# A convolution with dynamic per-channel weights on one core: the opening reordered, and the moments moved from GpSimd to TensorE and ScalarE

## The chip, the cores and the metric

The kernel runs on one core of a Trainium2 chip. The metric is the device time in microseconds of one execution, as the median of several. TensorE is written PE, VectorE DVE, ScalarE ACT, GpSimd POOL and SyncE SP, as in the profile. Each engine works through its own list of instructions in order and waits on semaphores; DMAs are all issued by SP.

## The reference

The input `x` has 16 images of 32 channels of 128x128, in float32. Each channel of each image is normalised over its pixels, then convolved 3x3 with a kernel of its own that is computed from the image's channel means, gated and added to the input:

```
v   = (x - mean(x)) / sqrt(var(x) + 1e-5)          # per image and channel
avg = v.mean(axis=(2, 3))
wk  = sigmoid(avg @ w1.T + b1)                      # 9 numbers per image and channel
y   = depthwise_conv3x3(v, wk, pad=1) + conv_bias
out = x + (v - y) * fscale * v + y
```

The mean of `v` is zero but for rounding; the kernel computes it nevertheless (`dev_mean`), since the reference's weights come from it.

## The kernel before, in words

**Layout.** A partition holds one row of 16-row blocks (stepped by 14 rows, so that neighbours overlap), a parity of columns and one of 4 slots of channels; the 32 channels are 8 groups of 4 slots. One image is 8 groups of 128x576 numbers (128x594 with margins). Everything below runs per image `i` and group `g`; a tile is one (i, g), and there are 128.

**The steady work of a tile.** ACT subtracts the mean in place (`centre`, L686) and later writes the linear part (`linear_part`, L722). PE does the convolution: 12 matmuls on 64x64 quarters of the array, 6 of 448 columns (`paired`, L435) and 6 of 128 (`halved`, L441), each run in two passes because the numbers are float32, into one of three PSUM tiles. DVE multiplies and adds out of PSUM (`product`, L582), which frees that PSUM tile: tile n starts on PE only when product n-3 is done. POOL adds the linear part for two groups at a time (`add_pair`, L852), and SP stores.

**The chain of an image.** Before tile (j, 0) can run, image j needs its statistics and its weights. DVE takes `bn` (L531) over each group and folds the pieces in `rows` (L538), for which ACT first scales the counts (`count`, L728). PE averages the row means (`mean_even`/`mean_odd`, L358/L364; `mean_whole`, L383, for images 0 and 1) and ACT negates them (`negative_mean`, L669). POOL then computes deviation, its square and the second moment (`second_moments`, L814, L817, L819). PE averages those (`spread_*`, L370, L377, L388), ACT copies them out (`copy_stats`, L690, L692), POOL takes the power -1/2 (`deviation`, L809) and lays out the averages (`average_columns`, L823, L825). PE spreads them (`averages`, L396, L411), ACT copies (`copy_averages`, L698), PE multiplies with the weights (`dynamics_*`, L404, L419, L427), ACT applies the sigmoid (L705), POOL scales (`scaled_taps`, L843), and DVE builds the 24 banded matrices for PE (`matrices`, L549, L556; for image 0 in four steps, `first_matrices`). PE's part of the chain for images i+1 and i+2 is put between the matmuls of image i by `chain(i, at)`: `at` is 2g before tile g, and 2g+1 in its middle.

**Order.** Nothing is planned at run time; the order on each engine is written out. For the steady images DVE alternates `bn(i+2 or i+3, .)` with `product(i, .)`, has `rows(i+2)` before product 2 and `matrices(i+1)` after product 4. In the opening DVE takes all of bn(0), rows(0), all of bn(1), rows(1), `first_matrices`, four of bn(2). PE waits for the constants before it does anything, and fills some gaps with idle matmuls (`keep_warm`, L497, 240 columns on 64 rows of the array). SP loads image 0 in four pieces, then the gates, the constants, the weights, images 1 to 4.

Of the kernel before, what the change touches and what calls it, by code (L numbers as in the profile page):

```python
# [13 lines left out]
TAPS = 3  # L14
# [20 lines left out]
WARM = 240  # L35

START_AHEAD, AHEAD = 4, 6
# [10 lines left out]
FIRST_LOADS = 4  # L48
# [6 lines left out]
for _name, _width in (("average", PARTS), ("band", TAPS * HALF), ("turn", TAPS),  # L55
                      ("spread", INPUTS), ("phase", PARTS), ("counts", 1)):
    _AT[_name] = (_N, _N + _width)
    _N += _width
# [13 lines left out]
def constants():  # L72
# [12 lines left out]
    put("average", same * new[:, None])  # L85
    put("counts", (row >= ROWS - STEP).astype(np.float32))
# [71 lines left out]
def build(nc, x, w1r, gate, const, out):  # L158
    with ExitStack() as ctx:
# [34 lines left out]
        row_stats = sb("row_stats", [PARTS, 2, GROUPS, 2])  # L194
        shift = sb("shift", [PARTS, 2, 2, GROUPS])
        moments = sb("moments", [PARTS, 2, GROUPS])
        square = sb("square", [PARTS, GROUPS])
# [26 lines left out]
        zstats_ps = stat_ps[:, GROUPS:3 * GROUPS]  # L224
        avg_ps = stat_ps[0:INPUTS, 128:128 + PARTS]
# [22 lines left out]
        dev_ready = sem("dev_ready")  # L248
        square_ready = sem("square_ready")
# [95 lines left out]
        def _(pe):  # L345
            pe.wait_ge(consts_loaded, 16)

# [4 lines left out]

            def mean_even(j):
                pe.wait_ge(rows_done, j + 1)
                for cols in (TOP, BOTTOM):
                    nc.tensor.matmul(stat_ps[cols, 0:GROUPS], average(TOP, cols), row_stats[TOP, j % 2, :, 0],  # L358
                                     start=True, stop=False).then_inc(mean_half, 1)

            def mean_odd(j):
                pe.wait_ge(mean_half, 2 * (j - 1))
                for cols in (TOP, BOTTOM):
                    nc.tensor.matmul(stat_ps[cols, 0:GROUPS], average(BOTTOM, cols), row_stats[BOTTOM, j % 2, :, 0],  # L364
                                     start=False, stop=True).then_inc(mean_done, 1)

            def spread_even(j):
                pe.wait_ge(moments_ready, j + 1)
                for cols in (TOP, BOTTOM):
                    nc.tensor.matmul(stat_ps[cols, GROUPS:3 * GROUPS], average(TOP, cols),  # L370
                                     moments[TOP].rearrange("p a g -> p (a g)"),
                                     start=True, stop=False).then_inc(zstats_half, 1)

            def spread_odd(j):
                pe.wait_ge(zstats_half, 2 * j)
                for cols in (TOP, BOTTOM):
                    nc.tensor.matmul(stat_ps[cols, GROUPS:3 * GROUPS], average(BOTTOM, cols),  # L377
                                     moments[BOTTOM].rearrange("p a g -> p (a g)"),
                                     start=False, stop=True).then_inc(zstats_done, 1)

            def mean_whole(j):
                pe.wait_ge(rows_done, j + 1)
                nc.tensor.matmul(mean_ps, const_of("average"), row_stats[:, j % 2, :, 0],  # L383
                                 start=True, stop=True).then_inc(mean_done, 1)

            def spread_whole(j):
                pe.wait_ge(moments_ready, j + 1)
                nc.tensor.matmul(zstats_ps, const_of("average"), moments[:].rearrange("p a g -> p (a g)"),  # L388
                                 start=True, stop=True).then_inc(zstats_done, 1)
# [4 lines left out]
            def averages_whole(j):  # L394
                pe.wait_ge(avg_cols_ready, j + 1)
# [71 lines left out]

            def chain(i, at):
                j = i + 1
                if j < B:  # L470
                    late = 3 if j <= 2 else 0
                    if at == 3 + late:
                        averages(j)
                    if at == 5 + late:
                        dynamics_first(j)
                    if at == 6 + late:
                        dynamics_second(j)
                if i == 0 and at == 1:
                    spread_even(1)
                if i == 0 and at == 2:  # L480
                    spread_odd(1)
                if i == 1 and at == 0:
                    spread_odd(2)
                j = i + 2
                if j < B:
                    if at == (11 if j == 2 else 9):
                        mean_even(j)
                    if at == (12 if j == 2 else 10):
                        mean_odd(j)
                    if at == (15 if j == 2 else 13):  # L490
                        spread_even(j)
                    if at == 14 and j > 2:
                        spread_odd(j)

            def keep_warm(count):
                for _ in range(count):
                    nc.tensor.matmul(conv_ps[:, CONV_TILES - 1, BANK:BANK + WARM], const_of("average")[0:HALF],  # L497
                                     cst[0:HALF, 0:WARM], start=True, stop=True)
# [28 lines left out]
        def _(dve):  # L527
# [6 lines left out]
            def rows(j):  # L534
                dve.wait_ge(pieces_done, GROUPS * (j + 1))
                dve.wait_ge(counted_ready, j + 1)
                for g in range(GROUPS):
                    ins = nc.vector.bn_aggr(row_stats[:, j % 2, g, :], pieces[:, j % 2, g].rearrange("p h s -> p (h s)"))  # L538
# [30 lines left out]
            def first_matrices():  # L569
                dve.wait_ge(tap_ready, 1)  # L570
                last_column(0)
                for k in range(PAIRS):
                    whole_triples(0, PAIR * k, PAIR * (k + 1))

# [39 lines left out]
            for i in range(B):  # L614
                nxt, stats = i + 1 < B, i + 2 < B
                if i == 0:
                    for g in range(START_AHEAD - 1):
                        bn(2, START_AHEAD + g)
                        product(0, g)
                    bn(2, GROUPS - 1)  # L620
                    product(0, 3)
                    rows(2)
                    bn(3, 0)
                    product(0, 4)
                    bn(3, 1)
                    product(0, 5)
                    bn(3, 2)
                    matrices(1)
                    product(0, 6)
                    bn(3, 3)  # L630
                    product(0, 7)
                    for g in range(4, AHEAD):
                        bn(3, g)
                else:
# [12 lines left out]
                    if nxt and i > 1:  # L647
# [4 lines left out]
                    if i == 1:  # L652
                        matrices(2)
# [8 lines left out]
        def _(act):  # L662
            act.wait_ge(ones_set, 1)
# [68 lines left out]
            count(0)  # L732
# [4 lines left out]
            centre(0, 1)  # L737
            centre(0, 2)
            copy_averages(0)
            centre(0, 3)  # L740
            centre(0, 4)
            sigmoid(0)
            count(1)
            for g in range(5, GROUPS):
                centre(0, g)
            negative_mean(1)
            fill_margins(1)
            for i in range(B):
                nxt, stats = i + 1 < B, i + 2 < B
                for g in range(GROUPS):  # L750
                    if nxt and g == (4 if i < 2 else 3):
                        copy_averages(i + 1)
                    if stats and g == (5 if i == 0 else 4):
                        count(i + 2)
                    if nxt and i > 1 and g == 5:
                        sigmoid(i + 1)
                    if stats and i > 0 and g == 6:
                        negative_mean(i + 2)
                        fill_margins(i + 2)
                    if i < 2 and g == 6:  # L760
                        sigmoid(i + 1)
                    if i == 0 and g == 7:
                        negative_mean(2)
                        fill_margins(2)
# [3 lines left out]
                    if i == 0 and g == 1:  # L768
                        copy_stats(1)
                    if i == 1 and g == 0:  # L770
                        copy_stats(2)
                    if stats and i > 0 and g == 7:
                        copy_stats(i + 2)

        @block.gpsimd
        def _(pool):
# [20 lines left out]
            pool.wait_ge(inv_ready, 1)  # L797
# [12 lines left out]

            def second_moments(j):
                pool.wait_ge(rows_done, j + 1)
                pool.wait_ge(neg_mean_ready, j + 1)
                nc.gpsimd.tensor_tensor(moments[:, 0], row_stats[:, j % 2, :, 0], neg_mean_of(j),  # L814
                                        ALU.add).then_inc(dev_ready, 1)
                pool.wait_ge(dev_ready, j + 1)
# [84 lines left out]
```

## Time and profile before

| what | value |
|---|---|
| median of 3 runs | 265.88 us (265.69 to 266.33) |
| the profiled execution's own time | 265.87 us |
| its span, first to last instruction | 263.9 us |
| busy in the span: PE, DVE, POOL, ACT | 235.7, 231.7, 227.6, 211.1 us |
| DMA, mean over the span | 295 GB/s |
| first convolution matmul | at 25.04 us |

The span is what the views below are measured in, from its own start; the time has about 2 us more around it. A busy PE is not a PE at its peak, since its matmuls overlap. An engine's busy share is an average over stages with different limits, so each stage has to be looked at by itself.

### The profile page before, as it was taken

The page shows a single profiled execution, that of the slowest core. Times are in us where ns is not written, and L with a number is a line of the kernel's source. Part 1 is how long each engine was busy: PE and PEld are TensorE (multiplying, and loading weights), DVE is VectorE, ACT ScalarE, POOL GpSimd, SP SyncE. Part 2 cuts the span into 40 slices and gives each one's busy share as a digit, 9 for nine tenths or more (in the row PEclk, how much of TensorE's full clock was granted, in tenths as well). Part 3 has the DMA queues.
Part 4 walks back from the last instruction along what each step waited for, and adds up shares of the span by engine and source line. Part 5 has one row for each costly group of instructions (what it writes and reads, how often), then busy time and mean ns, then how long its engine had stood idle before and what let it go on. Part 6 is the DMA issues. An engine that isn't in the chain of part 4 may idle for free.

```text
span 263.9 us, 9720 instructions
## 1 busy us (share of the span) xinstructions
PE 235.7 (89%) x3872; PEld 187.7 (71%) x3872; DVE 231.7 (88%) x552; ACT 211.1 (80%) x389; POOL 227.6 (86%) x259
## 2 busy tenths in 40 slices
PE   0069998989999999989999999999999999999991
PEld 0046875858788786878787887678787878888770
DVE  2886799999999999999999999899999999756655
ACT  2158789797898989797998989697989989899520
POOL 1261579899899999999999999999999999999982
PEclk9999999999999999999999999999999999999997
DMA  7999904696959989797979799797989733444476
GB/s 259 421 422 429 383 4 180 212 401 255 362 236 366 365 280 392 253 390 306 368 288 361 295 366 354 287 386 247 361 325 362 281 160 160 183 181 181 183 290 247
DMA packets 10413, 77.73 MB, mean 295 GB/s; under 512 B 1280, under 2 KB 1408, under 8 KB 2688
## 3 DMA queue, kind: packets, MB, share of 16 engines
q1 hardware_dynamic: 10368, 77.12, 75.8%
q8 instruction: 30, 0.49, 0.7%
q14 instruction: 15, 0.12, 0.1%
HBM read 39.37 MB, written 37.75 MB: 292 GB/s over the span
## 4 chain that ended last, share of the span: by engine, by line
PE 58%; DVE 23%; issue 10%; DMA 3%; ACT 2%; SPq 1%; POOL 1%; DVEq 0%; ACTq 0%; POOLq 0%
PE conv_ps L435 37%; PE conv_ps L441 13%; DVE outs L582 9%; DVE pieces L531 8%; DVE taps L549 4%; PE dyn_ps L419 3%; DMA w1s<-w1r 3%; PE dyn_ps L427 2%; PE conv_ps L497 1%; DVE taps L556 1%; ACT xs L686 1%; ACT linear L722 1%; DVE row_stats L538 1%; PE dyn_ps L404 1%; SPq L314 1%
## 5 line engine op out<-in xcount | busy, mean ns | idle before, releaser
L435 PE MATMUL conv_ps<-xs,taps 64*64 64x448 f32 x1536 | 219.9, 549 | 6.9 <-DVE outs L582 4.3
L852 POOL TENSOR_TENSOR outs<-outs,linear 128x1152 f32<-128x1152 f32 x63 | 166.1, 2647 | 1.0 <-DVE outs L582 0.7
L582 DVE SCALAR_TENSOR_TENSOR outs<-xs,beta,conv_ps 128x576 f32<-128x576 f32 x128 | 102.8, 805 | 20.3 <-PE conv_ps L435 19.6
L435 PEld LDWEIGHTS conv_ps<-xs,taps 64*64 64x64 f32 x1536 | 101.7, 133 | 26.6 <-issue 14.0
L441 PE MATMUL conv_ps<-xs,taps 64*64 64x128 f32 x1536 | 114.3, 272 | 0.6 <-issue 0.6
L722 ACT ACTIVATE linear<-xs,slope 128x576 f32<-128x576 f32 x128 | 109.0, 854 | 3.0 <-POOL outs L852 3.0
L531 DVE BATCH_NORM_STATS2 pieces<-xs 128x6 f32<-128x64 f32 (+1 forms) x256 | 102.2, 447 | 6.0 <-DMA xs<-x 6.0
L441 PEld LDWEIGHTS conv_ps<-xs,taps 64*64 64x64 f32 x1536 | 94.2, 133 | 9.3 <-issue 2.4
L686 ACT ACTIVATE xs<-xs,shift 128x594 f32<-128x594 f32 x128 | 99.2, 778 | 0.0
L809 POOL TENSOR_TENSOR inv_std<-numbers,minus_half 128x8 f32<-128x8 f32 x16 | 26.4, 1649 | 4.8 <-ACT dev_mean L692 4.6
L549 DVE TENSOR_TENSOR taps<-dyn_ps,tap 128x1512 f32<-128x1512 f32 (+1 forms) x19 | 27.8, 1477 | 0.0
L669 ACT ACTIVATE shift<-stat_ps 128x8 f32<-128x8 f32 x16 | 2.8, 177 | 16.8 <-PE stat_ps L364 15.3
L419 PEld LDWEIGHTS dyn_ps<-w1s,avg_rows 64*64 64x64 f32 x240 | 12.2, 132 | 4.7 <-issue 4.7
L538 DVE BATCH_NORM_AGGREGATE row_stats<-pieces 128x2 f32<-128x12 f32 x128 | 11.2, 158 | 3.2 <-ACT pieces L728 3.2
L419 PE MATMUL dyn_ps<-w1s,avg_rows 64*64 64x72 f32 x240 | 13.5, 225 | 0.0
L383 PE MATMUL stat_ps<-row_stats,cst 128*128 128x8 f32 x4 | 1.2, 364 | 12.9 <-DVE row_stats L538 12.9
L427 PEld LDWEIGHTS dyn_ps<-w1s,avg_rows 35*64 35x64 f32 x240 | 11.4, 133 | 0.8 <-issue 0.5
L383 PEld LDWEIGHTS stat_ps<-row_stats,cst 128*128 128x128 f32 x4 | 1.0, 310 | 13.5 <-issue 12.9
L427 PE MATMUL dyn_ps<-w1s,avg_rows 35*64 35x72 f32 x240 | 10.3, 222 | 0.0
L370 PEld LDWEIGHTS stat_ps<-moments,cst 64*64 64x64 f32 x60 | 6.7, 138 | 4.9 <-issue 2.0
L698 ACT ACTIVATE avg_rows<-stat_ps 99x128 f32<-99x128 f32 x16 | 6.5, 409 | 4.3 <-PE stat_ps L411 2.2
L411 PE MATMUL stat_ps<-cst,avg_cols 64*35 64x128 f32 (+1 forms) x60 | 10.0, 269 | 0.0
(59 smaller groups left out, 142.0 us busy)
## 6 DMA issues: line engine op xcount, KB each, us to landing
xs<-x SPq DMA_DIRECT2D x30, 1188.0 KB, 11.2
out<-outs SPq DMA_DIRECT2D x30, 1152.0 KB, 5.2
xs<-x SPq DMA_DIRECT2D x4, 594.0 KB, 6.0
out<-outs SPq DMA_DIRECT2D x3, 576.0 KB, 2.8
out<-outs SPq DMA_DIRECT2D x2, 288.0 KB, 2.6
cst<-const SPq DMA_DIRECT2D x1, 275.5 KB, 6.9
w1s<-w1r SPq DMA_DIRECT2D x1, 144.0 KB, 6.8
gates<-gate SPq DMA_DIRECT2D x1, 8.0 KB, 7.0
```

The costliest lines, as they stand in the source:

```text
L419: nc.tensor.matmul(sums_ps[cols], rows_of(TOP, s, cols), w1s[TOP, s], start=s == 0, stop=False).then_inc(dyn_half, 1)
L427: nc.tensor.matmul(sums_ps[cols], rows_of(rest, s, cols), w1s[rest, s], start=False, stop=s == SLOTS - 1).then_inc(dyn_done, 1)
L435: return nc.tensor.matmul(tile(i, g, taken)[:, START:BANK], taps[given, i % 2, at:at + HALF], xs[given, i % XBUFS, g, 0:PAIRED, 1 + shift: ...
L441: return nc.tensor.matmul(tile(i, g, half)[:, BANK:END], taps[half, i % 2, at:at + HALF], xs[half, i % XBUFS, g, PAIRED:BLOCKS, 1 + shift: ...
L531: ins = nc.vector.bn_stats(pieces[:, j % 2, g, k, :], xs[:, j % XBUFS, g, a:b, 1:1 + COLS])
L538: ins = nc.vector.bn_aggr(row_stats[:, j % 2, g, :], pieces[:, j % 2, g].rearrange("p h s -> p (h s)"))
L549: nc.vector.tensor_tensor(kept_of(j)[:, first:last, :, 0:TRIPLES * TAPS].rearrange("p g k (a q) -> p g k a q", q=TAPS), bands[:, :, 0:TRIP ...
L582: nc.vector.scalar_tensor_tensor(out=outs[:, i % OBUFS, g].rearrange("p (k w) -> p k w", w=COLS), in0=xs[:, i % XBUFS, g, :, 1:1 + COLS], ...
L686: nc.scalar.activation(whole, whole, ACT.Identity, bias=shift[:, j % 2, 1, g:g + 1]).then_inc(centred_ready, 1)
L722: nc.scalar.activation(linear[:, g], xs[:, i % XBUFS, g, :, 1:1 + COLS], ACT.Identity, bias=slope[:, i % 2, 1, g:g + 1], scale=slope[:, i ...
L809: nc.gpsimd.tensor_tensor(inv_std[:, j % 2], numbers[:, j % 2, VAR], minus_half[:], ALU.pow).then_inc(r_ready, 1)
L852: nc.gpsimd.tensor_tensor(tile, tile, linear[:, PAIR * k:PAIR * (k + 1)].rearrange("p g n -> p (g n)"), ALU.add).then_inc(out_ready, 1)
```

## The change

1. **Loads.** Image 0 is loaded in eight pieces instead of four.
2. **Idle matmuls from the start.** PE no longer waits for the constants first. From the landing of the first piece it runs nine idle matmuls of 176 columns on all 128 rows, one after each `bn(0, g)`; more of them stand between the steps of image 0's chain, up to two after waits of their own.
3. **Image 0's chain.** Its count is scaled by DVE (`first_count`) and no longer by ACT behind `turn_weights`; the averages are laid out by DVE (`first_averages`) between bn(1, 3) and bn(1, 4), and no longer by POOL; `rows(1)` comes after the first quarter of the matrices; three bn(2) instead of four stand before product (0, 0).
4. **Moments, for all images.** A second constant, `deviate` = identity minus `average`, gives PE the deviations of the row means directly, by two more matmuls beside each mean. ACT copies them and squares them out of PSUM (two more activations in `negative_mean`). The variances within rows are added by PE, in PSUM, by two more matmuls beside each spread. POOL's `second_moments` goes.
5. **Tables.** Where images 1 to 3 take their steps is in small tables; image 1's mean and spread go into image 0's tiles, and DVE's order for images 0 and 1 is written anew. From image 2's own loop on, the order is as before but for point 4.

```diff
-WARM = 240
+WARM = 176
-FIRST_LOADS = 4
+FIRST_LOADS = 8
...
+    put("deviate", np.eye(PARTS, dtype=np.float32) - same * new[:, None])
...
             def mean_even(j):
                 pe.wait_ge(rows_done, j + 1)
+                pe.wait_ge(zstats_copied, 2 * j)
                 for cols in (TOP, BOTTOM):
-                    nc.tensor.matmul(stat_ps[cols, 0:GROUPS], average(TOP, cols), row_stats[TOP, j % 2, :, 0],
+                    nc.tensor.matmul(mean_ps[cols], average(TOP, cols), row_stats[TOP, j % 2, 0],
                                      start=True, stop=False).then_inc(mean_half, 1)
+                for cols in (TOP, BOTTOM):
+                    nc.tensor.matmul(dev_ps[cols], deviate(TOP, cols), row_stats[TOP, j % 2, 0],
+                                     start=False, stop=False).then_inc(mean_half, 1)
...
+                    nc.tensor.matmul(zstats_ps[cols, GROUPS:], average(TOP, cols), row_stats[TOP, j % 2, 1],
+                                     start=False, stop=False).then_inc(zstats_half, 1)
...
+            MEAN = {1: (0, 1), 2: (0, 12), 3: (1, 11)}
+            SPREAD = {1: (0, 4), 2: (0, 15), 3: (1, 14)}
+            AVERAGES = {1: (0, 9), 2: (1, 7)}
+            DYNAMICS = {1: (0, 11), 2: (1, 9)}
...
+            first = xs[:, 0, 0].rearrange("p k w -> p (k w)")
+            pe.wait_ge(first_loaded[0], 16)
+            for g in range(GROUPS + 1):
+                at_least(pe, pieces_done, g)
+                keep_warm(first[:, 0:PARTS], first[:, 0:WARM], 1)
+            pe.wait_ge(consts_loaded, 16)
+            still = (const_of("average"), cst[:, 0:WARM])
             mean_whole(0)
+            keep_warm(*still, 1)
             spread_whole(0)
-            keep_warm(3)
-            pe.wait_ge(last_columns_set, 1)
+            keep_warm(*still, 4)
+            pe.wait_ge(r_ready, 1)
+            keep_warm(*still, 1)
             averages_whole(0)
+            keep_warm(*still, 1)
             dynamics_whole(0)
-            keep_warm(2)
-            mean_whole(1)
-            keep_warm(1)
+            keep_warm(*still, 2)
+            pe.wait_ge(sig_ready, 1)
+            keep_warm(*still, 1)
+            pe.wait_ge(tap_ready, 1)
+            keep_warm(*still, 1)
...
+            first_count()
+            rows(0)
             nc.vector.tensor_copy(band_ps, const_of("band")).then_inc(constants_set, 1)
-            rows(0)
...
-            for g in range(GROUPS):
+            for g in range(4):
                 bn(1, g)
+            first_averages()
+            for g in range(4, GROUPS):
+                bn(1, g)
+            dve.wait_ge(tap_ready, 1)
+            last_column(0)
+            first_matrices(0, 1)
             rows(1)
-            first_matrices()
-            for g in range(START_AHEAD):
+            first_matrices(1, PAIRS)
+            for g in range(3):
                 bn(2, g)
...
+                elif i == 1:
+                    for g in range(4):
+                        product(1, g)
+                        bn(3, 4 + g)
+                    rows(3)
+                    product(1, 4)
+                    bn(4, 0)
+                    product(1, 5)
+                    bn(4, 1)
+                    matrices(2)
...
             def negative_mean(j):
-                act.wait_ge(mean_done, j + 1 if j < 2 else 2 * j)
+                act.wait_ge(dev_done, 2 * j + 1)
                 nc.scalar.activation(neg_mean_of(j), mean_ps, ACT.Identity, scale=-1.0).then_inc(neg_mean_ready, 1)
+                nc.scalar.activation(moments[:, 0], dev_ps, ACT.Identity).then_inc(moments_ready, 1)
+                nc.scalar.activation(moments[:, 1], dev_ps, ACT.Square).then_inc(moments_ready, 1)
...
-            second_moments(0)
             fill_sides()
             deviation(0)
-            average_columns(0)
+            pool.wait_ge(inv_ready, 1)
+            pool.wait_ge(r_ready, 1)
             scales(0)
             scaled_taps(0)
-            second_moments(1)
```

DVE's new order in image 0 is product 0, bn(2, 3), then bn(2, 3+g) and product g for g = 1 to 4, rows(2), bn(3, 0), product 5, bn(3, 1), matrices(1), product 6, bn(3, 2), product 7, bn(3, 3).

## Rows read from the trace of the kernel before

**Rows 1.** Busy time by stretch: one steady image, and the last image.
```profile
86.36:100.81 14.45, 14.02 (x244) 11.50 (x245) 14.20 (x35) 13.01 (x25) 14.06 (x16) 1.00 0.88 330
245.18:257.20 12.02, 12.02 (x188) 8.79 (x190) 6.38 (x9) 4.80 (x6) 11.15 (x5) 1.00 0.62 256
```

**Rows 2.** The chain of waits in a steady image: start, us, what.
```profile
95.13 0.82 DVE outs L582
...
97.40 0.81 DVE taps L549
...
100.81 0.56 PE conv_ps L435
```

**Rows 3.** Timeline of POOL, the same step in two following images.
```profile
107.39 0.24 POOL L833 TENSOR_TENSOR numbers<-factors,inv_std 128x16 f32<-128x16 f32 x1
...
121.95 0.24 POOL L833 TENSOR_TENSOR numbers<-factors,inv_std 128x16 f32<-128x16 f32 x1
```

**Rows 4.** The line that loads image 0: issue and landing.
```profile
L314 SPq DMA_DIRECT2D xs<-x x4: 382/422/679, 0.7 to 2.1; - x4
...
DMA to landing us min/median/max: 4.5/6.0/7.5
```

**Rows 5.** Timeline of DVE in the opening, and one product of image 2.
```profile
5.22 5.99 DVE L531 BATCH_NORM_STATS2 pieces<-xs 128x6 f32<-128x64 f32 x16 [5.22 <-DMA xs<-x]
...
12.08 0.71 DVE L538 BATCH_NORM_AGGREGATE row_stats<-pieces 128x2 f32<-128x12 f32 x8 [0.61 <-ACT pieces L728]
...
13.71 5.86 DVE L531 BATCH_NORM_STATS2 pieces<-xs 128x6 f32<-128x64 f32 x16 [0.79 <-DMA xs<-x]
...
22.86 1.92 DVE L549 TENSOR_TENSOR taps<-dyn_ps,tap 128x378 f32<-128x378 f32 x4
...
29.78 0.81 DVE L582 SCALAR_TENSOR_TENSOR outs<-xs,beta,conv_ps 128x576 f32<-128x576 f32 x1 [1.39 <-PE conv_ps L435]
...
70.98 0.80 DVE L582 SCALAR_TENSOR_TENSOR outs<-xs,beta,conv_ps 128x576 f32<-128x576 f32 x1
```

**Rows 6.** The chain of waits in the opening.
```profile
12.94 0.58 PE stat_ps L383 x2
...
13.88 0.21 POOL moments L814
...
15.51 0.18 ACT dev_mean L692
...
15.82 1.68 POOL inv_std L809
...
18.35 0.73 PE stat_ps L396 x2
...
19.64 1.96 PE dyn_ps L404 x8
21.60 1.90 PE conv_ps L497 x4
...
25.11 0.36 PE conv_ps L435
```

**Rows 7.** Long matmuls (L435) by stretch of 1 us, with the granted clock.
```profile
25.00:26.00 1.00, 0.96 (x4) 0.29 (x4) 1.00 1.02 428
...
29.00:30.00 1.00, 1.00 (x13) 0.33 (x7) 1.00 1.04 437
```

**Rows 8.** Timeline of DVE: products in images 13 and 14.
```profile
224.60 0.81 DVE L582 SCALAR_TENSOR_TENSOR outs<-xs,beta,conv_ps 128x576 f32<-128x576 f32 x1 [0.75 <-PE conv_ps L435]
...
227.90 0.82 DVE L582 SCALAR_TENSOR_TENSOR outs<-xs,beta,conv_ps 128x576 f32<-128x576 f32 x1 [0.73 <-PE conv_ps L435]
...
234.27 0.81 DVE L582 SCALAR_TENSOR_TENSOR outs<-xs,beta,conv_ps 128x576 f32<-128x576 f32 x1 [0.84 <-PE conv_ps L435]
...
238.37 0.81 DVE L582 SCALAR_TENSOR_TENSOR outs<-xs,beta,conv_ps 128x576 f32<-128x576 f32 x1 [1.58 <-PE conv_ps L435]
...
241.63 0.82 DVE L582 SCALAR_TENSOR_TENSOR outs<-xs,beta,conv_ps 128x576 f32<-128x576 f32 x1 [0.69 <-PE conv_ps L435]
```

More of the change, by code:

```diff
@@ L54 @@
 _N = 0
-for _name, _width in (("average", PARTS), ("band", TAPS * HALF), ("turn", TAPS),
+for _name, _width in (("average", PARTS), ("deviate", PARTS), ("band", TAPS * HALF), ("turn", TAPS),
                       ("spread", INPUTS), ("phase", PARTS), ("counts", 1)):
@@ L473, in chain @@
+            def chain(i, at):
+                for j in range(i + 1, min(i + 3, B)):
+                    mean = MEAN.get(j, (j - 2, 9))
+                    spread = SPREAD.get(j, (j - 2, 13))
+                    dynamics = DYNAMICS.get(j, (j - 1, 5))
+                    if (i, at) == AVERAGES.get(j, (j - 1, 3)):
                         averages(j)
-                    if at == 5 + late:
+                    if (i, at) == dynamics:
                         dynamics_first(j)
-                    if at == 6 + late:
+                    if (i, at) == following(dynamics):
@@ L477, in chain @@
                         dynamics_second(j)
[L478 to L486, printed above, removed]
+                    if (i, at) == mean:
                         mean_even(j)
-                    if at == (12 if j == 2 else 10):
+                    if (i, at) == following(mean):
@@ L489, in chain, with keep_warm @@
                         mean_odd(j)
-                    if at == (15 if j == 2 else 13):
+                    if (i, at) == spread:
                         spread_even(j)
-                    if at == 14 and j > 2:
+                    if (i, at) == following(spread):
                         spread_odd(j)
-            def keep_warm(count):
+            def keep_warm(weights, moving, count):
                 for _ in range(count):
-                    nc.tensor.matmul(conv_ps[:, CONV_TILES - 1, BANK:BANK + WARM], const_of("average")[0:HALF],
-                                     cst[0:HALF, 0:WARM], start=True, stop=True)
+                    nc.tensor.matmul(conv_ps[:, CONV_TILES - 1, BANK:BANK + WARM], weights, moving, start=True, stop=True)
@@ L566, in matrices, with first_matrices, first_count, first_averages @@
                 last_column(j)
[L569 to L572, printed above, removed]
+            def first_matrices(first, last):
+                for k in range(first, last):
                     whole_triples(0, PAIR * k, PAIR * (k + 1))
+            def first_count():
+                dve.wait_ge(pieces_done, GROUPS)
+                nc.vector.tensor_scalar(pieces[:, 0, :, 1], pieces[:, 0, :, 1], const_of("counts"), None,
+                                        ALU.mult).then_inc(counted_ready, 1)
+            def first_averages():
+                dve.wait_ge(zstats_copied, 2)
+                dve.wait_ge(r_ready, 1)
+                nc.vector.tensor_tensor(avg[:], dev_mean[:], inv_std[:, 0], ALU.mult).then_inc(avg_ready, 1)
+                dve.wait_ge(avg_ready, 1)
+                nc.vector.tensor_tensor(avg_cols[:, 0:TAPS * C].rearrange("p (a g) -> p a g", g=GROUPS),
+                                        const_of("spread")[:, 0:TAPS * C].rearrange("p (a g) -> p a g", g=GROUPS),
+                                        avg[:].unsqueeze(1).to_broadcast([PARTS, TAPS * SLOTS, GROUPS]),
+                                        ALU.mult).then_inc(avg_cols_ready, 1)
             def product(i, g):
@@ L646, in _ @@
                     product(i, 4)
-                    if nxt and i > 1:
+                    if nxt:
                         matrices(i + 1)
@@ L736, in _ @@
             copy_stats(0)
-            centre(0, 1)
-            centre(0, 2)
+            for g in range(1, 5):
+                centre(0, g)
             copy_averages(0)
-            centre(0, 3)
-            centre(0, 4)
+            centre(0, 5)
             sigmoid(0)
+            centre(0, 6)
             count(1)
[L744 to L747, printed above, removed]
+            centre(0, 7)
+            COPY_STATS = {1: (0, 2), 2: (1, 1)}
+            COPY_AVERAGES = {1: (0, 4), 2: (1, 4)}
+            COUNT = {2: (0, 5), 3: (1, 5)}
+            SIGMOID = {1: (0, 6), 2: (1, 6)}
+            MEAN = {1: (0, 0), 2: (0, 7), 3: (1, 7)}
             for i in range(B):
-                nxt, stats = i + 1 < B, i + 2 < B
+                nxt = i + 1 < B
                 for g in range(GROUPS):
[L751 to L764, printed above, removed]
+                    for j in range(i + 1, min(i + 3, B)):
+                        if (i, g) == COPY_STATS.get(j, (j - 1, 0)):
+                            copy_stats(j)
+                        if (i, g) == COPY_AVERAGES.get(j, (j - 1, 3)):
+                            copy_averages(j)
+                        if (i, g) == COUNT.get(j, (j - 2, 4)):
+                            count(j)
+                        if (i, g) == SIGMOID.get(j, (j - 1, 5)):
+                            sigmoid(j)
+                        if (i, g) == MEAN.get(j, (j - 2, 6)):
+                            negative_mean(j)
+                            fill_margins(j)
                     linear_part(i, g)
@@ L868, in _ @@
                 add_pair(i, 0)
[L869 to L873 removed]
+                if nxt:
                     scaled_taps(i + 1)
                 add_pair(i, 1)
[L876 to L877 removed]
                 if stats and i > 0:
```

106 lines of the change are left out of this document (44 added, 62 removed).

## The prediction

> **What bounds the kernel now.** I read the busy time by stretch first, then the chain of waits, then each engine's timeline for the opening. A steady image takes 14.45 us, in which DVE is busy for 14.20, POOL 14.06 and PE 14.02 [rows 1]: three engines near their limit. The chain says which binds where: up to 95.1 it runs through PE (averages, dynamics, the long matmuls), at product 3 it goes over to DVE, through the matrices at 97.4 and product 5, whose end frees the PSUM tile with which PE starts the next image at 100.8 [rows 2]. So the cycle is half PE, half DVE. POOL's own turn is 14.56 (107.39 to 121.95) [rows 3], a tenth longer than the cycle; its lag grows, but no step of the cycle waits for it. A PE without statistics and dynamics needs 12.02 for 8 tiles, 1.50 each [rows 1].
>
> The opening is a single thread instead: each engine waits for the one before, the convolution starts at 25.1 [rows 6], and the first product is at 29.78 after a wait for PE of 1.39 [rows 5]. There the long matmuls run at half speed: 4 in 25 to 26, 13 in 29 to 30, while the clock row says 1.00 for both [rows 7]; I go by the matmuls, low level (1.2 GHz) before, 2.4 after. The idle matmuls before did not raise it.
>
> **Part by part: the opening.** (a) Loads. The first of four pieces lands 4.5 us after its issue at 0.7, the last 7.5 after 2.1, so 5.2 to 9.6, 1.48 apart [rows 4]. Eight pieces land 0.74 apart, the first at about 4.5, the last still at 9.6. DVE takes 5.99/8 = 0.75 a group [rows 5], so bn(0) ends 0.75 after the last landing, at 10.4 and not 11.2. Four more issues of 0.42 push those of gates, constants, weights and images 1 to 4 back by 1.7; their data queue behind image 0's until 9.6 anyhow, so zero, and up to 1.7 if that queue ran dry.
>
> (b) Count on DVE: rows(0) started at 12.08 after a wait of 0.61 for ACT [rows 5]. A small DVE step of 0.2 instead gives 10.7, ending at 11.4: 1.36 earlier.
>
> (c) Moments. Two passes of the mean took 0.58 from 12.94 [rows 6]; four take 0.7 to 1.1 by the clock, from 11.6: say 12.3. ACT's two new activations cost 0.18 each by `dev_mean`'s row [rows 6], so moments are there at 12.8; before, three POOL steps from 13.88 and PE's next start made it 14.7. Four passes of the spread end at 13.5. ACT still has the margins and one group to centre before it copies, at 14.0; POOL's power of 1.68 started at 15.82 [rows 6], now 14.45, ending at 16.1.
>
> (d) Averages on DVE stand behind bn(1, 0..3), whose data come at 13.71 [rows 5]: four groups of 0.73 end at 16.65, two small steps at 17.05. PE's part starts at 17.15 instead of 18.35 [rows 6]: of the lead of 1.4 from (c), 0.2 is lost.
>
> (e) Averages, copy and dynamics took 0.73, 0.5 and 1.96, and sigmoid with tap 0.6 to 22.25 [rows 6]. With the clock up I take 0.4, 0.5, 1.4 and 0.65: tap at 20.15. bn(1, 7) ends at 17.05 + 4 x 0.73 = 20.0, so DVE hardly waits. Last column and first quarter: 0.6, done at 20.75; before, at 23.4 (22.86 and a quarter of 1.92 [rows 5]). PE starts at 20.9: 4.1 sooner.
>
> (f) What that is worth is read where both orders have done the same DVE work again: product 5 of image 2, at 70.98 [rows 5], since DVE's order is the old one from there on. From 23.4 to it were 47.6 us, of which 2.4 were waits (1.39 at product 0, the rest small): 45.2 of work. The new order adds rows(1), 0.65, behind the first quarter: 45.85, without waits at 66.6. The waits I find by walking the tables with PE at 1.50 a tile and DVE at 1.45 for a bn and a product. Averages(1) at (0, 9): image 1's mean is done at 22.75, ACT needs 1.0 for it and the margins and 1.44 for each of two rounds of linear part and centring, so it copies at 26.7; POOL's power ends at 28.8, the columns are there at 29.65, and PE stands 0.75, of which product 4 feels 0.35. Between products 4 and 5 of image 0 PE has a tile (1.50), the dynamics (1.1), a wait for rows(2) and a mean, 3.0 together, DVE only 2.15: 0.85. In image 1, which PE starts at 38.25, bn(3, 7) ends at 47.2, count and rows(3) at 48.3; mean_even(3) at (1, 11) stands in PE's queue from 47.6 and holds the rest of tile 5, so product 5 comes 1.05 late. Sum 2.25, so 68.85: **a gain of 2.1**. Bounds: no waits 4.4; twice these waits, -0.1.
>
> **The steady images.** POOL loses three steps, some 0.8 from 13.88 to PE's start at 14.7 [rows 6]; no step of the cycle waits for POOL, so zero, and at most what DVE leaves idle, 0.25 an image [rows 1]. ACT gains 0.36 and is busy 13.01 of 14.45: covered by its idle time. If that cover went, the centred groups of the next image would come late, but they are a whole image ahead. PE gets 8 more passes with the mean (at 9 and 10) and 8 with the spread (13, 14). The second set lies where DVE sets the pace: zero, hidden by matrices and products. The first lies between product 3 and product 4, which wait for PE. How dear is it? With a mean, products 2 to 4 of image 13 took 227.90 - 224.60 = 3.30; without, in image 14, 241.63 - 238.37 = 3.26 [rows 8]: 8 passes cost 0.04. From the other side, products 0 to 4 of image 14 took 7.36, against 4 x 1.50 = 6.0 [rows 8, 1], so its 36 passes of averages and dynamics cost 0.038 each, 8 cost 0.30. I take 0.08, near the row of the same place and shape, a little above since the queue in one quarter of the array doubles. Images 3 to 12, ten times: 0.8; image 13, with nothing left to hide behind, 0.2 more. **Cost 1.0**, bounds 0.5 and 3.4.
>
> The Trainium skill speaks against this step (TensorEngine Tiling (Array Packing), Instruction Overhead): each matmul carries some 60 cycles however few its columns. As an estimate from that page, 8 passes would cost 0.2 us an image and the sum would end at 266.0; the product rows above show a fifth of that.
>
> On the clock the TensorE: Matmul & The Clock Gate page (Part 1) says that throttled is the default and activity releases it. By it nine matmuls on the full array would do what (e) assumes; the trace agrees as far as the convolution goes, not for the half-array idle matmuls before it, and no row shows the full-array ones.
>
> **Sum.** The profiled execution took 265.87, span 263.9, against a median of 265.88. 265.87 - 2.1 + 1.0 = **264.8**.
>
> **Rivals.**
> 1. *PE never holds DVE, or POOL's relief counts.* Speaks for it: POOL's turn of 14.56 is the longest. Against: nothing waits for POOL. Gain 4.4 - 1.0 gives 262.5; POOL's 0.25 x 10 with (f) as it is gives 262.3.
> 2. *The clock is low in the chain* (slower). The dynamics then take 1.96; idle matmuls cost about 0.65 each (0.95 now, two in 1.90 [rows 6], by 176/240). Four stand after the dynamics, ahead of the convolution in PE's queue: PE starts at about 23.1, and with the 4.7 from 25.1 to 29.78 the first product is at 27.8, 1.9 before the old one but with two bn(2) of 0.73 fewer done. 0.5 is gained, and the 1.0 more of waits that the new tables have is lost: -0.6, hence 267.4. It decides if the long matmuls of image 0's first tile take twice their time. For it: the clock did not rise before 28 in the trace. Against: the new idle matmuls use all rows and start at 4.5.
> 3. *Each pass costs its mean*, 0.30 an image: 3.4 in all, 267.2 at the same opening. Product 4 must start 0.3 later after product 2 than now. Against: the product rows.
> 4. *No effect*: moved steps hit other waits, and (f) brings only the 1.0 that PE's passes cost, 265.9.
>
> **Chances.** What can be told from no change here is 0.3%, 0.8 us: 265.1 to 266.7. The forecast 0.42 (its own range 264.0 to 265.9; faster 0.27, same 0.15); rival 1 0.20, all faster; rival 2 0.20 (slower 0.16, same 0.04); rival 3 0.10 (slower 0.06, same 0.04); rival 4 0.08, same. Together faster 0.47, same 0.31, slower 0.22. The range reaches from rival 1 to rival 2, 262.3 to 267.4.
>
> **What would show it.** rows(0) done by 11.5 and the first convolution matmul near 20.9 with short matmuls; product 5 of image 2 at 68 to 70; a steady cycle of 14.5 to 14.6, and POOL with gaps before `deviation`. The forecast falls if the convolution starts after 22.5, if a wait of over 1 us before an L435 or L582 stands in images 0 and 1 that I have not listed, or if the cycle changes by more than 0.2.

## The result and the profile after

The changed kernel takes **268.26 us** (median of 4 runs, 267.49 to 268.75) against 265.86 of the kernel before (4 runs): ratio 1.0098, 95% interval 1.0074 to 1.0122. It is 1% slower, and above the widest range that the prediction gave (262.3 to 267.4). The profiled execution took 268.75 us with a span of 266.9, 3.0 more than before. Medians here and below are over all runs, while ratios leave out those in a slower state of the chip (two of e3a, two of e5 and one of e6, whose medians without them are 265.26, 264.13 and 263.23 us).

The opening first: timeline of DVE of the changed kernel.

```profile
10.97 0.26 DVE L601 TENSOR_SCALAR pieces<-pieces,cst 128x48 f32<-128x48 f32 x1
11.26 0.71 DVE L564 BATCH_NORM_AGGREGATE row_stats<-pieces 128x2 f32<-128x12 f32 x8
...
14.20 2.98 DVE L558 BATCH_NORM_STATS2 pieces<-xs 128x6 f32<-128x64 f32 x8 [1.61 <-DMA xs<-x]
...
17.28 0.26 DVE L609 TENSOR_TENSOR avg_cols<-cst,avg 128x96 f32<-128x96 f32 x1
...
20.57 0.54 DVE L575 TENSOR_TENSOR taps<-dyn_ps,tap 128x378 f32<-128x378 f32 x1
...
25.15 0.80 DVE L621 SCALAR_TENSOR_TENSOR outs<-xs,beta,conv_ps 128x576 f32<-128x576 f32 x1
...
32.03 0.81 DVE L621 SCALAR_TENSOR_TENSOR outs<-xs,beta,conv_ps 128x576 f32<-128x576 f32 x1 [0.30 <-PE conv_ps L449]
...
34.91 0.81 DVE L621 SCALAR_TENSOR_TENSOR outs<-xs,beta,conv_ps 128x576 f32<-128x576 f32 x1 [0.76 <-PE conv_ps L449]
...
47.92 0.71 DVE L564 BATCH_NORM_AGGREGATE row_stats<-pieces 128x2 f32<-128x12 f32 x8 [0.46 <-ACT pieces L785]
...
51.11 0.81 DVE L621 SCALAR_TENSOR_TENSOR outs<-xs,beta,conv_ps 128x576 f32<-128x576 f32 x1 [1.06 <-PE conv_ps L449]
...
68.89 0.79 DVE L621 SCALAR_TENSOR_TENSOR outs<-xs,beta,conv_ps 128x576 f32<-128x576 f32 x1
```

The steps up to the first matrices end 0.3 to 0.6 us later than forecast (the passes of the spread, not shown, 1.0). Product 5 of image 2, which sums them up, is at 68.89: 68.85 was forecast, and before it was at 70.98 [rows 5]. So 2.1 us were won by there. The same stretch on PE:

```profile
3.50 2.58 PE L513 MATMUL conv_ps<-xs 128*128 128x176 f32 x6 [3.50 <-DMA xs<-x]
6.91 4.94 PE L513 MATMUL conv_ps<-xs 128*128 128x176 f32 x12 [0.82 <-DVE pieces L558]
...
18.70 1.08 PE L418 MATMUL dyn_ps<-w1s,avg_rows 99*128 99x72 f32 x8
19.62 1.44 PE L513 MATMUL conv_ps<-cst 128*128 128x176 f32 x8
21.17 0.97 PE L449 MATMUL conv_ps<-xs,taps 64*64 64x448 f32 x4
...
69.99 0.60 PE L449 MATMUL conv_ps<-xs,taps 64*64 64x448 f32 x4 [1.19 <-issue]
```

The dynamics take 1.08 instead of 1.96 [rows 6]. The last line is a stall of 1.19 us in image 2 for which the profile shows no releaser; it comes right after the point at which the gain was read.

Then the steady image: busy time in one image (us; the numbers are PE, PEld, DVE, ACT, POOL), and DVE's timeline in it.

```profile
86.36:101.25 14.89, 14.89 (x265) 12.23 (x261) 14.21 (x35) 13.06 (x27) 13.64 (x13) 1.00 0.77 283
```

```profile
92.95 0.82 DVE L621 SCALAR_TENSOR_TENSOR outs<-xs,beta,conv_ps 128x576 f32<-128x576 f32 x1
...
94.70 0.82 DVE L621 SCALAR_TENSOR_TENSOR outs<-xs,beta,conv_ps 128x576 f32<-128x576 f32 x1 [0.21 <-PE conv_ps L449]
...
96.69 0.81 DVE L621 SCALAR_TENSOR_TENSOR outs<-xs,beta,conv_ps 128x576 f32<-128x576 f32 x1 [0.44 <-PE conv_ps L449]
97.42 1.73 DVE L575 TENSOR_TENSOR taps<-dyn_ps,tap 128x1512 f32<-128x1512 f32 x1
```

The cycle is 14.89 instead of 14.45 [rows 1]. DVE has the same 14.2 of work; POOL has less. Products 2 to 4 take 96.69 - 92.95 = 3.74, and the matrices start right behind product 4. PE is "busy" all 14.89 us, against 14.02 of 14.45 before, and that row does not say where the time goes. The loads of its weights say more. For reading them: the even rows lie in one half of the array's rows, the odd rows in the other, so each quarter of the array takes one parity in and gives one out. A cross convolution goes from one parity to the other, `own_parity` (448 columns, of the tile before) from each to itself, and the even half of the mean and of the deviations comes right behind `own_parity`. Here are the loads around the mean, before and after:

```profile
94.02 0.14 PEld L435 LDWEIGHTS conv_ps<-xs,taps 64*64 64x64 f32 x2
94.04 0.13 PEld L358 LDWEIGHTS stat_ps<-row_stats,cst 64*64 64x64 f32 x1
94.07 0.14 PEld L435 LDWEIGHTS conv_ps<-xs,taps 64*64 64x64 f32 x2
94.37 0.13 PEld L358 LDWEIGHTS stat_ps<-row_stats,cst 64*64 64x64 f32 x1 [0.15 <-issue]
94.37 0.19 PEld L435 LDWEIGHTS conv_ps<-xs,taps 64*64 64x64 f32 x2
94.45 0.13 PEld L358 LDWEIGHTS stat_ps<-row_stats,cst 64*64 64x64 f32 x1
```

```profile
93.59 0.20 PEld L449 LDWEIGHTS conv_ps<-xs,taps 64*64 64x64 f32 x4
93.70 0.45 PEld L358 LDWEIGHTS stat_ps<-row_stats,cst 64*64 64x64 f32 x3
94.39 0.13 PEld L358 LDWEIGHTS stat_ps<-row_stats,cst 64*64 64x64 f32 x1 [0.24 <-issue]
94.39 0.13 PEld L361 LDWEIGHTS stat_ps<-row_stats,cst 64*64 64x64 f32 x1
94.41 0.13 PEld L449 LDWEIGHTS conv_ps<-xs,taps 64*64 64x64 f32 x1
```

Both begin with the weights of `own_parity` (two matmuls in two passes each). Before, the next cross convolution's weights follow 0.35 later (94.02 to 94.37). They even come ahead of the third load of the mean (94.45), which stands before them in the program. After, they follow 0.82 later (93.59 to 94.41), behind the first load of the deviations (L361). My reading is that they are held up there, since a second small matmul must wait for the quarter in which `own_parity` runs; the experiments d1 to e5 test it.

The account of the 3.0 us of span, from tile starts in both traces: opening -2.1; the stall in image 2 +1.2; images 3 to 12 ten times +0.44; image 13 14.58 instead of 13.73, +0.85; image 14 -0.2; and -1.25 for delays of 0.26 and 0.99 that the execution before had in images 5 and 9. That makes 2.9.

### The profile page after: what moved, and what is told of

Its sections match the earlier page's. It is cut to its first block, busy times and chain, and to the rows that moved or that the text cites. A ratio compares the mean times of both kernels' runs of the same rounds, so it can differ in the third digit from the quotient of the medians.

```text
span 266.9 us, 10250 instructions
## 1 busy us (share of the span) xinstructions
PE 253.1 (95%) x4150; PEld 201.3 (75%) x4150; DVE 232.6 (87%) x555; ACT 211.5 (79%) x420; POOL 218.5 (82%) x209
## 4 chain that ended last, share of the span: by engine, by line
PE 84%; DVE 5%; issue 4%; DMA 3%; SPq 2%; ACT 1%; POOL 1%; DVEq 0%; ACTq 0%
PE conv_ps L449 54%; PE conv_ps L455 20%; PE dyn_ps L433 3%; DMA xs<-x 3%; PE dyn_ps L441 2%; DVE pieces L558 2%; SPq L314 1%; DVE outs L621 1%; PE stat_ps L384 1%; POOL inv_std L858 1%; PE stat_ps L361 1%; PE stat_ps L358 1%; DVE outs L631 1%; PE stat_ps L376 0%; PE stat_ps L370 0%
## 5 line engine op out<-in xcount | busy, mean ns | idle before, releaser
L449 PE MATMUL conv_ps<-xs,taps 64*64 64x448 f32 x1536 | 232.7, 548 | 2.6 <-DVE taps L582 1.3
L449 PEld LDWEIGHTS conv_ps<-xs,taps 64*64 64x64 f32 x1536 | 108.3, 132 | 20.3 <-issue 7.0
L455 PEld LDWEIGHTS conv_ps<-xs,taps 64*64 64x64 f32 x1536 | 93.0, 132 | 5.9 <-issue 0.9
L858 POOL TENSOR_TENSOR inv_std<-numbers,minus_half 128x8 f32<-128x8 f32 x16 | 26.4, 1648 | 22.1 <-ACT dev_mean L749 22.1
L433 PE MATMUL dyn_ps<-w1s,avg_rows 64*64 64x72 f32 x240 | 14.1, 226 | 0.0
L564 DVE BATCH_NORM_AGGREGATE row_stats<-pieces 128x2 f32<-128x12 f32 x128 | 11.2, 161 | 0.5 <-ACT pieces L785 0.5
L513 PE MATMUL conv_ps<-xs 128*128 128x176 f32 x18 | 7.5, 580 | 4.3 <-DMA xs<-x 3.5
L358 PEld LDWEIGHTS stat_ps<-row_stats,cst 64*64 64x64 f32 x60 | 6.1, 132 | 6.4 <-issue 2.7
L425 PE MATMUL stat_ps<-cst,avg_cols 64*64 64x128 f32 (+1 forms) x60 | 10.1, 270 | 0.4 <-POOL avg_cols L864 0.4
L513 PEld LDWEIGHTS conv_ps<-xs 128*128 128x128 f32 x18 | 4.5, 312 | 6.9 <-DMA xs<-x 3.5
L376 PEld LDWEIGHTS stat_ps<-moments,cst 64*64 64x64 f32 x60 | 4.8, 132 | 6.2 <-issue 6.2
```

The lines of the kernel that those rows point to most:

```text
L433: nc.tensor.matmul(sums_ps[cols], rows_of(TOP, s, cols), w1s[TOP, s], start=s == 0, stop=False).then_inc(dyn_half, 1)
L449: return nc.tensor.matmul(tile(i, g, taken)[:, START:BANK], taps[given, i % 2, at:at + HALF], xs[given, i % XBUFS, g, 0:PAIRED, 1 + shift: ...
L455: return nc.tensor.matmul(tile(i, g, half)[:, BANK:END], taps[half, i % 2, at:at + HALF], xs[half, i % XBUFS, g, PAIRED:BLOCKS, 1 + shift: ...
L858: nc.gpsimd.tensor_tensor(inv_std[:, j % 2], numbers[:, j % 2, VAR], minus_half[:], ALU.pow).then_inc(r_ready, 1)
```

## The experiments

Below, "cycle" is the time from one image's first convolution matmul to the next's, in images without a stall. A "pass" is one of the two records that the traces show for each matmul (1536 for the 128 x 6 long ones); all matmuls here are float32, so that the type is the reason is not shown. Comments in the code shown are mine.

| kernel | time, us | ratio to before, 95% interval | cycle | products 2 to 4 |
|---|---|---|---|---|
| before | | | 14.45 | 3.29 |
| changed | 268.26 | 1.0098 (1.0074 to 1.0122) | 14.89 | 3.74 |
| e1 POOL's moments | 263.65 | 0.9925 (0.9890 to 0.9960) | 14.45 | 3.29 |
| e2 only point 4 | 272.94 | 1.0272 (1.0250 to 1.0295) | 14.89 | |
| e3a no deviations | 265.97 | 0.9962 (0.9932 to 0.9993) | 14.45 | 3.30 |
| e3b no row variances | 270.28 | 1.0164 (1.0104 to 1.0224) | 14.89 | |
| d1, d2, d3 | 266.00, 265.26, 264.75 (one run each) | | 14.77, 14.61, 14.56 | 3.63, 3.46, 3.41 |
| e5 mean at 8 and 10 | 264.24 | 0.9956 (0.9916 to 0.9997) | 14.51 | |
| e6 as e5, from image 5 | 263.52 | 0.9905 (0.9876 to 0.9935) | 14.51 | 3.36 |
| e7 e1 with e6's places | 262.86 | 0.9891 (0.9864 to 0.9917) | 14.41 | 3.26 |
| e8 e1, no idle matmuls | 266.27 | 1.0018 (1.0003 to 1.0034) | 14.45 | |
| e9 before, idle matmuls | 263.87 | 0.9926 (0.9896 to 0.9956) | 14.45 | |

**Opening or steady images? (e1, e2)** e1 gives images 4 and later the moments by POOL again.

```diff
+                if j >= J0:          # J0 = 4: no deviations beside the mean, no row variances beside the spread
+                    return
...
+                if stats and i + 2 >= J0:
+                    second_moments(i + 2)
```

> The changed opening, but from image 4 on the moments are POOL's again, as in the kernel before: four passes of the mean and four of the spread on TensorE, no copy and square on ScalarE. Theory A (the opening keeps its 2.1 us, and the whole loss is the passes put into the steady images, about 0.45 us each): a steady cycle of 14.45 us and 263.8 us, or up to 265.0 if the stall without a releaser in image 2 comes again. Rival B (the new opening leaves the images in a worse order, and the loss is that): the cycle stays at 14.9 and the time at 267 to 268.5 us.

263.65 us, cycle 14.45: theory A to 0.2 us. The new opening costs nothing in later images. e2 is the converse, the kernel before with point 4 alone from image 3 on.

> The opening of the kernel before, and from image 3 on the moments by TensorE and ScalarE as in the changed kernel. Theory A: eleven images of 0.45 us, 270.5 us (269.5 to 271.3), a steady cycle of 14.9. Rival B: nothing of the new opening is in it, so 266 to 266.9 us (the prediction's own price of the passes, 1.0 us, is its upper end) and a cycle of 14.45 to 14.55.

272.94 us, cycle 14.89 from image 2's loop on. The cycle is A's; the time is 1.6 above its range. In the profiled execution image 0 took 0.8 longer (the trace's record of the full clock begins at 30.09 us there, at 28.68 in the kernel before), and images 8 to 10 lost 2.0 in stalls, of which the largest again had no releaser:

```profile
PE conv_ps L458 <- issue: 1.2, 1, 1.2
```

**Which passes? (e3a, e3b)**

```diff
 def mean_even(j):
...
+                if j >= J0:
+                    return
                 for cols in (TOP, BOTTOM):
                     nc.tensor.matmul(dev_ps[cols], deviate(TOP, cols), row_stats[TOP, j % 2, 0],
...
```

This is e3a, and `mean_odd` is shortened in the same way; e3b leaves the matmuls over `row_stats` out of `spread_even` and `spread_odd`.

> The changed kernel without the four deviation matmuls beside the mean from image 4 on: the deviations of the row means that ScalarE copies and squares there are those of image 3, the four spread passes over row_stats stay. Theory A1 (the four passes beside the mean set the cycle, since they delay tiles 4 and 5, the product of tile 4 and with it the matrices; the spread's are hidden by the wait for a product behind them): a cycle of 14.45 to 14.55, 264 to 265 us. Theory A2 (each of the eight passes costs its share): 14.65, 266 us. Rival C (ScalarE's copy and square make the cycle longer): 14.9, 268 us.

> The changed kernel without the four spread passes over row_stats from image 4 on: the variances within the rows are left out of the spread there. Theory A1: a cycle of 14.8 to 14.9 and 267.5 to 268.3 us, and the wait for a product behind the spread grows from 0.33 to about 0.8 us. Theory A2: 14.65, 266 us. Rival C: 14.9, 268 us.

Without the deviations the cycle is 14.45, with the row variances still there and ScalarE still copying and squaring. Without the row variances it stays 14.89. So the four matmuls beside the mean are the whole price in a steady image, and the spread's are hidden; C falls, A1 holds. The new wait of `mean_even` for the copied statistics (`zstats_copied`) is still in e3a, so it costs nothing either. Both times are above A1's by more than the cycles explain, e3b's with two runs alone (269.01 and 271.56); the profiled executions had waits without a releaser of 3.1 us (e3a) and 3.3 us (e3b) together, all before image 7. An image without one, in e3a and in e3b:

```profile
175.17:189.62 14.45, 14.45 (x256) 11.88 (x252) 14.20 (x35) 13.07 (x28) 13.65 (x13) 1.00 0.91 339
```

```profile
176.40:191.29 14.89, 14.43 (x257) 11.81 (x253) 14.21 (x35) 13.09 (x27) 13.69 (x13) 1.00 0.87 318
```

**Their number, or their place? (d1, d2, d3, e5)** e1 with extra matmuls from image 4 on:

```diff
+                    for cols in (TOP,):          # d1; d2: (BOTTOM, BOTTOM); both behind the even half of the mean
+                        nc.tensor.matmul(dev_ps[cols], deviate(TOP, cols), row_stats[TOP, j % 2, 0],
+                                         start=False, stop=False).then_inc(mean_half, 1)
...
+                    for cols in (TOP, BOTTOM):   # d3, behind the odd half
+                        nc.tensor.matmul(dev_ps[cols], deviate(BOTTOM, cols), row_stats[BOTTOM, j % 2, 0],
+                                         start=True, stop=True).then_inc(dev_done, 1)
```

> The version with the changed opening and POOL's moments from image 4 on (steady cycle 14.45 us), with one matmul more behind the even half of the mean: a deviation from the even rows to the even rows, the quarter of TensorE in which the parity's own convolution of the tile before still runs; its result is not read. Theory H1 (a second small matmul for a busy quarter holds up all that stands behind it in TensorE's queue): this one alone gives most of the 0.45 us, a tile pitch of 2.0 to 2.1 us instead of 1.73 and a cycle of 14.8 to 14.9. Theory H3 (each matmul more costs its share, an eighth to a quarter of 0.45 us): 14.5 to 14.55.

> The same version with two matmuls more in the same place, both from the even rows to the odd rows, the quarter whose convolution is over sooner; their result is not read. H1: little, a pitch of 1.73 to 1.85 us and a cycle of 14.45 to 14.55. H3: two shares, a cycle of 14.55 to 14.7, more than with the one matmul.

> The same version with two matmuls more behind the odd half of the mean, half a tile later, from the odd rows to either parity; their result is not read. H1: a cycle of 14.45 to 14.5, since the convolutions of the half tile before are short there and no quarter is long busy. H3: two shares, 14.55 to 14.7.

One matmul for the quarter of `own_parity` lengthens the cycle by 0.32 us; two for the cross quarter by 0.16, two behind the odd half by 0.11, so 0.08 and 0.055 each on average. H1 holds in its main point: one in the wrong quarter costs four to six times one elsewhere, and more than two of them, against H3. But d1 is 0.03 under H1's range, and the cycles of d2 and d3 lie in the ranges of H3 and not of H1: a plain price of each matmul is real, only small. The set in the changed kernel, one of the first kind, one of the second and two of the third, adds up to 0.51 and measured 0.44. The weight loads of d1 show the same idle time at the place, 0.24 us:

```profile
122.33 0.21 PEld L366 LDWEIGHTS stat_ps<-row_stats,cst 64*64 64x64 f32 x2 [0.15 <-issue]
122.79 0.13 PEld L366 LDWEIGHTS stat_ps<-row_stats,cst 64*64 64x64 f32 x1 [0.24 <-issue]
122.79 0.14 PEld L472 LDWEIGHTS conv_ps<-xs,taps 64*64 64x64 f32 x2
```

e5 keeps all matmuls of the changed kernel and moves only the place:

```diff
-                    mean = MEAN.get(j, (j - 2, 9))
+                    mean = MEAN.get(j, (j - 2, 8))     # and mean_odd at (j - 2, 10)
```

> The changed kernel with all its matmuls, only the even half of the mean moved one half tile earlier for images 4 on: both halves of it stand ahead of a tile's first cross pair, where no own-parity convolution has just been issued. H1: a pitch of 1.5 to 1.8 us there, a cycle of 14.45 to 14.55 us, and 262.5 to 264 us. H3: the same passes at the same cost, 14.9 and 268 us. Rival: the row statistics come too late for the earlier place, and TensorE waits for them for some tenths of a microsecond each image.

A cycle of 14.51, as H1 expected, and 264.24, 0.24 above its range: 0.38 of the 0.44 us an image are gone with the same passes. The rival shows too, but once: in image 2 the tile with the mean took 1.2 us longer, and PE waits for the row statistics.

```profile
PE stat_ps L358 <- DVE row_stats L564: 1.5, 2, 0.9
```

e6 leaves that one mean in its old place (`MEAN[4] = (2, 9)`):

> The changed kernel with the two halves of the mean ahead of a tile's first cross pair as in the run before, but for image 4, whose mean stays in its old place (the row statistics came 0.9 us late there). Theory H1: the 1.2 us that image 2 lost there come back but for the 0.45 of the old place, cycles of 14.5 us from image 3 on, 263.2 to 263.8 us. Rival: the row statistics are late in image 2 wherever the mean stands, and 264.2 us stays.

263.52, as expected: with two places moved the changed kernel is 1% faster than the kernel before. e7 moves them in e1:

> The changed opening, POOL's moments from image 4 on, and the mean's four matmuls in the earlier place from image 5 on. If tile pitches in this stretch set the cycle by way of the product behind the mean: 14.35 to 14.4 us and 262.5 to 263.3 us. If the vector engine's own work sets it (14.24 us of 14.45 busy) or the matrices wait for something else: 14.45 and 263.6 us.

262.86 and a cycle of 14.41, the first expectation: the best of all here, 1.1% below the kernel before.

**What in the opening brings the gain? (e8, e9)** e8 is e1 with `keep_warm` empty. e9 is the kernel before with the idle matmuls of the changed one and the waits they stand behind, nothing else.

> The changed opening and POOL's moments from image 4 on, without the idle matmuls that TensorE runs in the opening. Theory A (a good part of the opening's gain is TensorE's clock): mean, averages and dynamics take half as long again to twice as long, the first convolution starts 1 to 1.5 us later, its first tile takes 3.8 us instead of 2.2, and the time is 265 to 266.7 us. Rival (image 0 is set by VectorE's products and matrices, so that a slow clock there is hidden): 263.7 to 264.2 us.

> The kernel before with nothing changed but the idle matmuls of the opening: those of the changed kernel (128 rows by 176 columns, from the arrival of image 0 on, and behind each step of its chain). Theory A (the opening's gain is TensorE's clock above all): its steps and the first tile take the short durations, the first convolution starts at 23 to 24 instead of 25.0 us, the first tile takes 2.2 to 2.5 instead of 3.8 us, and the time is 263.5 to 264.3 us. Rival (the chain on VectorE and the new order are needed for it, since image 0's pace is set by them): 265.0 to 266 us.

Both came out as A, but for e9's first convolution, which came still earlier, at 22.57. Without idle matmuls the new opening loses 2.6 us (266.27 against 263.65, from two series; 2.5 by the ratios) and is no faster than the old one; the idle matmuls alone give the old one 2.3 (266.2, the kernel before beside it, to 263.87), as much as the whole new opening. First e8 (line, count, busy us, mean ns; then a window of its long matmuls; then its first product), then PE of e9:

```profile
L438 PE MATMUL dyn_ps<-w1s,avg_rows 99*128 99x72 f32 x8 | 2.0, 426 | 0.6 <-ACT avg_rows L775 0.6
```

```profile
24.00:25.00 1.00, 1.00 (x4) 0.36 (x4) 1.00 1.00 418
```

```profile
27.87 0.81 DVE L639 SCALAR_TENSOR_TENSOR outs<-xs,beta,conv_ps 128x576 f32<-128x576 f32 x1 [1.81 <-PE conv_ps L469]
```

```profile
19.12 1.08 PE L400 MATMUL dyn_ps<-w1s,avg_rows 99*128 99x72 f32 x8
...
22.57 0.97 PE L431 MATMUL conv_ps<-xs,taps 64*64 64x448 f32 x4
```

In e8 the dynamics take 2.0 us and 4 long matmuls start in a microsecond, the low level (1.2 GHz), where the changed kernel has 10 in 25 to 26, and product 0 waits 1.81 for PE. In e9 the dynamics take 1.08, the high level (2.4 GHz). The clock row says 1.00 in all these windows. The packed traces tell why: their records of the clock begin at 28.68 us in the kernel before, 28.37 in e8 and 17.17 in the changed kernel, and the views show a stretch without a record as 1.00. In the kernel before, the long matmuls take 0.95 to 1.00 us up to 27.6 and 0.54 from 28.87 on, on either side of that record. So ahead of the first record the durations have to be read. In e9 the records are 1.00 from 11.16 to 14.58, 0.50 to 17.99 and 1.00 from there; from 11.2 to 14.5 PE was busy for 1.40 of 3.30 us. Product 5 of image 2 is at 68.19 in e9, earlier than the 68.89 of the changed kernel, though its first product is later (26.91 against 25.15): the waits of the new tables in images 0 and 1 take back what the chain on VectorE wins.

## Why the prediction was wrong

- **The opening, (a) to (f): right in its sum**, to 0.04 us at the place where it was to be read. The three waits named in (f), 0.35, 0.85 and 1.05, came as 0.30, 0.76 and 1.06. The 0.04 is luck in part: image 1's data, whose delay (a) put at zero, came at 14.20 and not 13.71; the first quarter of the matrices ended 0.36 late; two waits of 0.46 and 0.18 stood on no list; and DVE had some 0.8 less work than the 45.85 taken.
- **Its reason was half the story.** The text gave the gain to shorter steps on VectorE as much as to the clock. In e9 the idle matmuls alone bring as much as the whole new opening in e1 (0.9926 and 0.9925), and e8, the new opening without them, brings nothing (1.0018). Rival 2, the low clock, did not occur. Its price, 267.4 - 264.8 = 2.6, is near what e8 lost, though e8 has no idle matmuls in PE's way, and the "about 0.65" for one of them is 0.70 by the rows it names (0.95 x 176/240).
- **The failed step is the first set of passes in the steady images**: "I take 0.08, near the row of the same place and shape". It is 0.44 an image, more than five times that, 4.4 us in the ten images for which 0.8 was taken. The place was right: the passes lie between product 3 and product 4, and products 2 to 4 took 3.74 instead of 3.29. The size was wrong. The rows used, products of image 13 against image 14 [rows 8], gave 0.04 and compared two images on DVE; on PE, tiles 3 to 5 start 3.27 us apart in image 13 and 3.06 in image 14, a difference of 0.21 for the mean's four matmuls. And the text named what makes the new ones dearer ("the queue in one quarter of the array doubles") without following what stands behind that queue: the tile's second pair of cross convolutions, then product 4, the matrices, product 5 and the next image. d1 measured 0.32 for the one matmul in that quarter, and e5 got 0.38 back by the place alone.
- **Rival 3** ("each pass costs its mean", 0.30 an image) had the right sign and place, and nearly the price of a plain matmul: 0.038 a pass is 0.076 a matmul, against 0.055 in d3 and 0.08 in d2. On these the Trainium skill (TensorEngine Tiling (Array Packing), Instruction Overhead) is right too: some 60 cycles, 0.05 us for two passes as an estimate. Neither gives the 0.32 of the one matmul behind a long one in its own quarter.
- **The second set, beside the spread, zero: right** (e3b) but in image 13, where 0.2 was taken in all and 0.85 measured; the mean's passes alone give 0.45 of it (14.18 in e3b).
- **POOL and ACT, zero: right.** POOL now waits 22.1 us for its input and the cycle gained nothing by it; e1, with POOL's steps back, has the old cycle.
- The stall in image 2 was no part of any theory. Such stalls stand in ten of the fourteen executions profiled here, at changing places.

## What to carry to other kernels

A small matmul may be priced by where it stands in PE's queue: here the same 8 columns cost 0.32 us behind a long matmul in their own quarter of the array and 0.055 to 0.08 elsewhere. So before such work is taken out again, try another place for it: half a tile earlier gave back 0.38 of its 0.44 us. Where steps are moved and idle work is added in one change, run the idle work alone: here it was the whole gain. And read a cost on the engine that does the work, on one place with and without it.

## What the runs showed of the hardware that was not expected

- The quarters of TensorE run out of step: a cross convolution's weights were loaded at 94.37, ahead of the mean's third load at 94.45, which stands before them in the program. But they do not pass everything: d1 against d2 shows the price of the quarter (0.32 and 0.08). That all loads come from one queue, in which one set of weights can wait per quarter and the next blocks, is read from the order of the loads and not shown.
- Idle matmuls of 128 rows by 176 columns, the first nine from 3.5 us on, brought the short durations by the dynamics at 18.7, where the kernel before still had the long durations at 25 to 26 [rows 6, 7]. The Trainium skill (TensorE: Matmul & The Clock Gate, Part 1) has activity release the clock; the runs agree.
- PE stops now and then for 0.3 to 1.2 us with no releaser in the profile. The traces hold a lead that no run here tested: all 16 such waits of over 0.3 us behind the opening, in the 14 traces, end 1.2 to 1.6 us after a transfer of 16 KB on queue 8, which the page calls "instruction", has landed. There are 30 to 33 of these transfers in an execution, about one every 7 us, and most are followed by no stop. So the fetching of PE's instructions is the first suspect; the cause stays open.
